# Who copies the index lists for the gathers and scatters of a mixture of experts

## What is computed

```
mod = (silu(c) @ wmod): shift, scale, gate of either half, per batch
h = layernorm(x) * (1 + scale_a) + shift_a
x = x + gate_a * attention(h)              # 16 heads of 16, 4 key/value heads
h = layernorm(x) * (1 + scale_b) + shift_b
probs = softmax(h @ router_w.T)            # 8 experts
w = the largest probs of each token until their sum passes 0.9, others 0
for e in range(8):
    y = (silu(h @ gate_w[e].T) * (h @ up_w[e].T)) @ down_w[e].T     # 256 -> 512 -> 256
    out = out + y * w[:, e]
x = x + gate_b * out
```

## Time and profile before

| | us |
|---|---|
| median of 3 runs | 476.06 |
| lowest and highest of them | 474.22, 476.64 |
| the profiled execution, its own time | 476.70 |
| its span, first to last instruction | 475.1 |
| TensorE busy | 438.7 |
| VectorE busy | 333.2 |
| ScalarE busy | 257.9 |
| GpSimd busy | 194.1 |

### The profile page before, as it was taken

How to read it: one execution, slowest core, us unless ns; L and a number is a source line. 1 busy time by engine, 2 the same in 40 slices (tenths; PEclk the granted TensorE clock), 3 DMA queues, 4 the chain that set the end, 5 groups by cost and what they waited for, 6 DMA issues and landing times. The chain is left out here.

```text
span 475.1 us, 10022 instructions
## 1 busy us (share of the span) xinstructions
PE 438.7 (92%) x3466; PEld 328.3 (69%) x3466; DVE 333.2 (70%) x770; ACT 257.9 (54%) x372; POOL 194.1 (41%) x233
## 2 busy tenths in 40 slices
PE   7988889998999899999999899999999999999992
PEld 7453232343444334437998899899899999999992
DVE  3688885698779967688988677484566475756542
ACT  2276889777877788785342354353353353533330
POOL 4142023032002200011535665766656655776755
PEclk8899999999999999999999999999999999999997
DMA  8701307710011002134275368557538565654443
GB/s 257 243 1 53 83 2 88 91 46 1 1 48 44 1 2 90 38 99 135 63 218 117 75 154 207 117 121 171 112 68 210 92 179 124 122 95 102 81 80 45
DMA packets 30785, 46.01 MB, mean 97 GB/s; under 512 B 3588, under 2 KB 22276, under 8 KB 30728
## 3 DMA queue, kind: packets, MB, share of 16 engines
q0 software_dynamic: 11936, 22.50, 26.7%
q1 hardware_dynamic: 18792, 22.77, 14.9%
HBM read 34.44 MB, written 12.93 MB: 100 GB/s over the span
## 5 line engine op out<-in xcount | busy, mean ns | idle before, releaser
L681 ACT ACTIVATE probs<-psS 128x1024 f32<-128x1024 f32 x128 | 123.6, 1033 | 15.2 <-PE psS L1569 15.1
L1812 PE MATMUL psS<-hs_hi,w_hi 128*128 128x256 f32 x400 | 113.2, 283 | 3.7 <-DVE hs_lo L1317 2.2
L1812 PE MATMUL psS<-hs_lo,w_hi 128*128 128x256 f32 x400 | 112.3, 281 | 0.0
L1812 PE MATMUL psS<-hs_hi,w_lo 128*128 128x256 f32 x400 | 112.2, 280 | 0.0
L526 POOL DMA_INDIRECT out<-y_sel,idx_out x44 | 76.9, 1748 | 36.4 <-DVE y_sel L1357 24.9
L1812 PEld LDWEIGHTS psS<-hs_hi,w_hi 128*128 128x128 f32 x400 | 75.3, 188 | 5.1 <-issue 5.1
L1812 PEld LDWEIGHTS psS<-hs_hi,w_lo 128*128 128x128 f32 x400 | 75.3, 188 | 0.0
L1812 PEld LDWEIGHTS psS<-hs_lo,w_hi 128*128 128x128 f32 x400 | 75.3, 188 | 0.0
L512 POOL DMA_INDIRECT h_sel<-h_rows,idx_in x50 | 53.9, 1078 | 42.0 <-DVE sel L1323 17.2
L1672 PE MATMUL psY<-probs,v_aug 128*32 128x512 f32 x512 | 68.2, 605 | 0.0
L740 ACT ACTIVATE silu_g<-psS 128x512 f32<-128x512 f32 x50 | 29.8, 598 | 59.4 <-PE psS L1812 56.2
(11 more groups left out here) (229 smaller groups left out, 688.7 us busy)
## 6 DMA issues: line engine op xcount, KB each, us to landing
w_in<-gateT SPq DMA_DIRECT2D x8, 512.0 KB
w_in<-upT SPq DMA_DIRECT2D x8, 512.0 KB
w_in<-downT SPq DMA_DIRECT2D x8, 512.0 KB
h_rows<-h_nat SPq DMA_DIRECT2D x4, 528.0 KB
x_all<-x SPq DMA_DIRECT2D x4, 512.0 KB, 5.5
h_rows<-mod_table POOLq DMA_DIRECT2D x4, 512.0 KB
out<-x_all SPq DMA_DIRECT2D x4, 512.0 KB, 2.9
mod_rows<-mod_table SPq DMA_DIRECT2D x3, 512.0 KB, 5.3
```

What stands on the lines that cost most here:

```text
L681: act.activation(probs[:, gk % 4, 2 * pair:2 * pair + 2, :], psS[:, pair, :, :], ACT.Exp, scale=ATT_SCALE / QK_UNIT ** 2).then_inc(probs_d ...
L1812: mm = pe.matmul(ps[:, i * SW:(i + 1) * SW], w, v[:, k, :], start=at == 0, stop=at == 3 * KC - 1)
```

## The change

The two small copies of an item go from GpSimd to VectorE, and earlier in the walk: read_list(m + 2) stands in VectorE's item m behind split_input(m + 1), and write_list(m - 1) behind output(m - 1). VectorE, no longer GpSimd, waits for idx_ready, and for one list further. The first list of the walk, read_list(5), stands behind rows_of_places(2) in the order written out by hand, write_list(2) behind output(2, 2). The early items keep GpSimd's copies; so does the last item of all (idx_last). GpSimd's gather also increments a semaphore, rows_free, for which nothing waits.

```diff
--- before.py
+++ after.py
@@ -250,9 +250,9 @@
 
         (w_rounded, w_ready, gate_ps, up_ps, silu_ready, a_ready, a_rounded, a_split, down_ps, turned, sel_hi, sel_lo,
          w_copied, tiles_listed, in_listed, out_listed, last_listed, last_ps, last_ready, gathered, scattered,
-         y_ready) = sems(
+         y_ready, rows_free) = sems(
             "w_rounded w_ready gate_ps up_ps silu_ready a_ready a_rounded a_split down_ps turned sel_hi sel_lo "
-            "w_copied tiles_listed in_listed out_listed last_listed last_ps last_ready gathered scattered y_ready")
+            "w_copied tiles_listed in_listed out_listed last_listed last_ps last_ready gathered scattered y_ready rows_free")
         block = ctx.enter_context(nc.Block())
 
         w_src = [w.rearrange("e (k p) n -> e p k n", p=P) for w in (gateT, upT, downT)]
@@ -507,6 +507,7 @@
                 pool.wait_ge(in_listed, m)
                 pool.wait_ge(turned, m)
                 pool.wait_ge(w_copied, m)
+                pool.sem_inc(rows_free, 1)
                 rows = LAST * N if isinstance(m, int) and m < EARLY else T
                 for k in range(S):
                     pool.indirect_dma_start(h_sel[:, k, :], None, h_rows[0:rows, :],
@@ -553,13 +554,8 @@
             scatter(1)
 
             def body_of_item(e, first, m):
-                if first:
-
-                    pool.wait_ge(idx_ready, min(e + 2, E))
-                pool.wait_ge(in_listed, m)
-                read_list(m + 1)
+
                 gather(m + 1)
-                write_list(m - 2)
 
                 scatter(m - 2, y_last if e == 0 and first else y_sel)
 
@@ -567,7 +563,6 @@
             pool.wait_ge(x2_out, 16 * B)
             items = pool.value_load(meta[0:1, 2, E - 1:E], min_val=EARLY + E, max_val=EARLY + ITEMS)
             walk_items(pool, body_of_item, lambda e, before: None)
-            write_list(items - 2)
 
             pool.tensor_copy(idx_last[:, :], idx_all[:, bass.ds(S * (items - 1), S)]).then_inc(last_listed, 1)
             scatter(items - 2)
@@ -1323,6 +1318,16 @@
                 dve.tensor_scalar(sel[:, bass.ds(m % RING, 1), :, 1:].rearrange("p o k e -> p (o k) e"), h_sel[:, :, C:ROW], 0.0,
                                   None, ALU.add).then_inc(w_copied, 1)
 
+            def read_list(m):
+
+                dve.wait_ge(gathered, 32 * m)
+                dve.tensor_copy(idx_in[:, :], idx_all[:, bass.ds(S * m, S)]).then_inc(in_listed, 1)
+
+            def write_list(m):
+
+                dve.wait_ge(scattered, GATES + 32 * m)
+                dve.tensor_copy(idx_out[:, :], idx_all[:, bass.ds(S * m, S)]).then_inc(out_listed, 1)
+
             def product(m, h):
                 dve.wait_ge(silu_ready, 2 * m + h + 1 + FREE)
                 dve.wait_ge(up_ps, 2 * m + h + 1)
@@ -1413,7 +1418,10 @@
                 take_weights(4)
                 tiles_of_places(EXPERTS0, E)
                 rows_of_places(2)
+                dve.wait_ge(idx_ready, 2)
+                read_list(EARLY + 1)
                 output(2, 2)
+                write_list(2)
                 split_hidden(3, 0)
                 split_hidden(3, 1)
 
@@ -1422,12 +1430,17 @@
                 take_weights(m + 1)
                 product(m, 1)
                 split_input(m + 1)
+                if first:
+
+                    dve.wait_ge(idx_ready, min(e + 3, E))
+                read_list(m + 2)
                 split_hidden(m, 0)
 
                 if first:
                     output(e or EXPERTS0, m - 1, before_walk=e == 0)
                 else:
                     output(1 + e, m - 1)
+                write_list(m - 1)
                 split_hidden(m, 1)
 
             def between_experts(e, before):
```

## The result

The change makes the kernel slower: 481.69 us in the median of four runs (480.96 to 483.5) against 475.17 us, a ratio of 1.0139 with a 95% interval of 1.0112 to 1.0167. It was measured again later with five rounds: 483.9 against 475.71 us, 1.0174 (1.013 to 1.0218). The loss is thus some 6.6 to 8.3 us, where 2.4 us were forecast. The direction was right, and 481.69 lies inside the range of 475 to 483, near its end; the size was wrong by a factor of about three, and the second median lies outside.

A forecast was written before the change was run, and what follows sets the result against it. TensorE, busy 438.7 us of a 475.1 us span, was taken as the bound. First list +3.0, steady gathers +0.7, relieved waits -1.4 and tail +0.1 gave +2.4 on 476.06: 478.5 us, range 475.0 to 483.0.

The forecast's parts named there:

- the first list: Start of the walk: read_list(5) behind rows_of_places(2) makes gather 5 3.06 us late, all reaching TensorE; +3.0 us, bounds 2.3 to 3.6.
- The periods with a list have 1 us more and absorb it: Six items where TensorE also makes a list: period about 10 us against 9.1, so later gathers cost nothing there.
- the steady part: Gathers in the walk become later; 3 to 4 of 14 plain periods lose 0.2 us: +0.7 us, bounds 0 and 2.5.
- The chain to a gather: Each walk item: turn, hs_hi, hs_lo, list, release; the gather's first DMA starts 2.94 us after the turn's start.
- the four lags that I took: From a gather's second DMA to its first waiting user: 3.99, 4.62, 3.95 and 4.56 us, used to forecast landings.
- the two relieved waits: Turns at 308.90 and 405.15: gathers start earlier without GpSimd's copy; gain 1.4 us of 2.12, bounds 0.7 and 2.12.
- "issue" in front: Gather for the turn at 405.15: 1.70 us marked "issue" may stay if GpSimd's own fetching, leaving some 0.6 us.
- 14 periods that I called plain: Of the walk's 20 periods, those without a list made by TensorE, taken as 9.1 us each.
- the tail: End of the kernel: the idx_out copy follows the last y_sel on VectorE; +0.1 us, bounds 0 and 0.3.
- VectorE's copies: In the walk: 42 copies at 0.16 us, taken from a 163 ns cast, 7 us on VectorE, costing 0.
- rival A: List chain late in every plain item: some 0.35 us lost in each of 14 periods, +5 us, 482.8 us; chance 0.2.
- The rule that I weighed: VectorE's SBUF copies stop GpSimd writing descriptors: 0.3 us an item, gain 0.8 for 1.4, sum +3.0, time 479.1 us.

The follow-up runs named there:

- the first experiment: The changed kernel with read_list(5) moved directly behind take_weights(4), ahead of tiles_of_places and rows_of_places(2): 478.97 us, 1.0037 of the kernel before.
- the second profile: Profile of the changed kernel run once more, unaltered, beside the kernel before: 483.9 us, 1.0174.

## Why the prediction was right or wrong

**The mechanism of the first list was right, its size too small.** VectorE's fixed order delayed gather 5 and all of the delay reached TensorE, as two experiments show in both directions. The term was +3.0 us, bounds 2.3 to 3.6; the direct part is 3.61 between the first two profiles. The gather was 3.09 us late for a forecast of 3.06; then its first DMA was slowed by 1.05 us beside VectorE's subtractions, where at most 0.3 us stood in the bounds. But the profile of before that I compared with had its clock at 1.00 ahead of turn 5. Against the other profile of that kernel (11.57 us) the late turn costs only 2.64 us, since a late gather hides what the lower clock costs ahead of it. Up to turn 6 the changed kernel takes 26.26 and 25.86 us from turn 4, the kernel before 20.71 and 21.61 us: 4.3 to 5.6 us more, where 3.0 were forecast. That is also what the first experiment took back, 4.9 to 6.5 us.

**A term was missing.** I passed a wait of 3 to 4 us to the end of the kernel at its own length. It also took TensorE's clock, and 1.94 us of the next period with it (12.05 for 10.11; 1.5 us in the second profile). No rival held this step, from a wait to its cost. The experiment with TensorE at work shows that the idle time took the clock; it does not isolate the term in the time.

**"The periods with a list have 1 us more and absorb it" was the step that failed in the steady part.** The chain to a gather was right where it was reckoned. GpSimd and VectorE show it for the gathers of items 11 and 12, with turns at 322.57 and 333.82 above:

```profile
323.70 0.68 DVE L1335 TENSOR_TENSOR a_full<-psS,silu_g 128x512 f32<-128x512 f32 x1
...
325.24 0.68 DVE L1312 TENSOR_TENSOR hs_lo<-psM,hs_hi 128x512 fp32r<-128x512 f32 x1
325.84 0.15 DVE L1324 COPY idx_in<-idx_all 128x2 int32 x1
...
335.13 0.69 DVE L1312 TENSOR_TENSOR hs_lo<-psM,hs_hi 128x512 fp32r<-128x512 f32 x1
335.74 0.16 DVE L1324 COPY idx_in<-idx_all 128x2 int32 x1
```

```profile
326.86 1.03 POOL L513 DMA_INDIRECT h_sel<-h_rows,idx_in  x1 [2.76 <-DVE idx_in L1324]
328.19 0.98 POOL L513 DMA_INDIRECT h_sel<-h_rows,idx_in  x1 [0.30 <-issue]
...
336.76 1.02 POOL L513 DMA_INDIRECT h_sel<-h_rows,idx_in  x1 [2.48 <-DVE idx_in L1324]
```

In a plain item the gather starts at 336.76, 2.94 us after its turn: exactly the forecast. But behind the weight splits VectorE comes to hs_lo only at 325.24, the list is ready at 325.99, and the gather starts at 326.86, 4.29 us after its turn (2.92 before). Its second DMA, at 328.19, has its user waiting until 333.82, 5.63 us, longer than any of the four lags that I took. The extra microsecond of the period was used up and TensorE waited 1.01 us. The same chain stands behind waits of 1.29, 1.02 and 1.14 us at turn 11 in three of the experiments.

With 0.7 lost and 1.4 gained I had forecast a gain of 0.7 us from turn 6 on; the profile shows a loss of 1.80. Of the two relieved waits, 1.19 us became 0.47 and 0.93 became 0.72: a gain of 0.9, not 1.4; the gather for turn 19 still had 2.12 us of "issue" in front, as the prediction feared. And of the 14 periods that I called plain two were longer in the kernel before as well (10.42 and 9.60 us, to turns 13 and 14). The experiments agree with this as the place: with the lists of those items early too, the rest of the loss is gone.

The waits at turns 11 and 18 change from one profile of the same code to the next (1.01 and 0.28, then 1.18 and 0.95), and the second profile has a scatter of 5.72 us in front of turn 11; how much of the 1.80 us is the list chain and how much such scatters is not settled. Nor is the 1.80 us itself firm. From turn 6 to turn 25, where their code is the same, four profiles took 182.06, 182.37, 182.72 and, with TensorE kept awake, 179.54 us; the kernel before took 180.26 and 179.12. In that fourth profile the gather for turn 11 starts as late (4.28 us after turn 10), but its rows were there 4.73 us or less after its second DMA, not 5.6 to 5.9 as in four others, and nothing waited. So at turn 11 the late list cost time only where the transfer was slow too, and what makes it slow is open.

Put together, the profile's 6.7 us is the forecast 2.4, plus 0.6 for the first list, 1.9 for the clock, 2.5 for the steady part and 0.1 for the tail, less 0.85 between executions.

**The tail was right:** 0.2 us for 0.1, with bounds of 0 and 0.3. VectorE's copies cost 0.16 us into idx_in, as reckoned from the cast, and 0.19 us into idx_out (medians of 22 each, 44 in all for 42 reckoned), and no wait of TensorE for them appeared.

**The rivals.** A (late in every plain item) is nearest in time, but not in cause: the plain items with no delay before lost next to nothing. The rule that I weighed was about copies, and the slowing that I read as agreeing with it (1.54 us at 302.43) stood beside a subtraction of two SBUF operands; it was no sign of that rule. The long DMAs of the experiments stand beside such instructions too: no row shows a moved copy holding a DMA up, but a scatter that starts beside VectorE's large blocks can last until 1.5 us after their end.

That the measured 481.69 us lies in the range owes something to luck. The range had no term for the lower clock; it reached so far up for rival A, late gathers in every plain item, which did not happen. The second median is outside it.

## What to carry to other kernels

- A small copy that moves to another engine takes that engine's place in the order. Look first at its first instance, behind the hand-written prologue, and then at the items where that engine has its large blocks; the mean item says little.
- A wait of several microseconds on TensorE can cost more than its length: behind waits of 2.53, 4.00 and 3.98 us here the granted clock was down and the period 1.5 to 2.3 us longer, behind one of 2.21 us it was not. Price both. Idle products in the wait keep the clock, but they help only if they end with it, and they must stand where the wait is, not behind it.
- Where the copy is made as soon as its data are there, the change costs nothing that can be told here; it gains nothing either, since the relieved engine did not set the end.

## What the runs showed of the hardware

- TensorE idle for 4.0 us: clock 0.50 afterwards and 1.94 us lost in the next period. Kept busy with 36 transposes in the same place: clock 1.00 and a next period of 10.04 us. Idle for 2.1 us ahead of the walk: clock 0.50 behind it in nine of 14 profiles. Idle for 2.21 us in front of turn 8 in one profile: clock 1.00 and a next period of 9.00 us.
- An indirect scatter's first DMA on GpSimd took 1.6 us alone; beside a block of VectorE instructions with two SBUF operands it took 2.3 to 2.4 us when it started 0.3 to 0.4 us into the block, 1.8 us when it started 0.9 us or more into it, and in nine cases of 84 it took 4.7 to 5.8 us, ending 1.5 us after the block in all nine (358.54 for 357.04 above).
